# Two additions per unit become one, the context product moves to the start, and loads and products of the first units are reordered

## What is computed

```python
h = gelu(gelu(cond @ W0 + b0) @ W1 + b1)
att = softmax(h @ W2 + b2)                       # (64, 8)
c = einsum('boi,bih->boh', att @ weight, x) + att @ bias_k
q, k, v = c @ Wq, c @ Wk, c @ Wv                 # with their biases; 32 values per row, 32 heads for q only
o = softmax(q * k / sqrt(32)) @ v                # per row; 32 values
x = x + repeat(o, 32 times each)                 # 32 -> 1024 channels
y = conv1d(x, weight, 9 taps, 4 groups) + cond @ c_weight.T + bias
out = x + y @ (scale * (unpack4(packed) - zero)).T + ffn_bias
```

## Time and profile before

| | |
|---|---|
| median of 3 runs | 431.62 us (431.26 to 432.72) |
| the profiled execution | 432.14 us, its span 430.2 us |
| mean granted TensorE clock | 0.992 |
| PE busy | 412.6 us (96%) |
| DVE busy | 363.5 us (85%) |
| POOL busy | 340.9 us (79%) |
| ACT busy | 226.8 us (53%) |
| DMA | 79.05 MB, mean 184 GB/s |

### The profile page before, as it was taken

One profiled execution on the slowest core, in us unless ns is written; L12 is line 12 of the kernel. 1 busy time (PEld: TensorE's weight loads), 2 busy tenths in 40 slices (PEclk: granted clock), 3 DMA queues, 4 the chain that ended last, 5 costly groups with the idle time before them and its releaser, 6 DMA issues.

```text
span 430.2 us, 6661 instructions
## 1 busy us (share of the span) xinstructions
PE 412.6 (96%) x2195; PEld 348.8 (81%) x2195; DVE 363.5 (85%) x603; ACT 226.8 (53%) x465; POOL 340.9 (79%) x316
## 2 busy tenths in 40 slices
PE   3969899899999999999999999999999999999997
PEld 2969799778888888888888888888888888888885
DVE  2896999998989899899989799998989799983421
ACT  3854655556455274657446365647264465562700
POOL 4033948769686999999999979899979979999920
PEclk9988999999999999999999999999999999999999
DMA  8989246470637565664736290928174371816112
GB/s 312 385 330 379 102 149 225 146 270 5 182 106 265 192 220 202 181 240 143 281 100 223 62 350 20 329 88 259 63 237 185 69 254 38 287 41 234 48 52 98
DMA packets 21752, 79.05 MB, mean 184 GB/s; under 512 B 5704, under 2 KB 5832, under 8 KB 17352
## 3 DMA queue, kind: packets, MB, share of 16 engines
q1 hardware_dynamic: 21416, 77.21, 51.2%
q10 hardware_dynamic: 288, 1.18, 0.9%
HBM read 61.11 MB, written 17.27 MB: 182 GB/s over the span
## 4 chain that ended last, share of the span: by engine, by line
PE 79%; DVE 6%; DMA 2%; issue 1%; POOL 1%; ACT 0%; DVEq 0%; POOLq 0%
PE p_f L1159 51%; PE p_conv L1153 19%; PE p_sm L1129 7%; PE p_sm L1138 1%; DMA o_c<-o_dram 1%; DMA o_dram<-o_sb 1%; DVE den L837 1%; DVE c_lo L882 1%; DVE xc L876 1%; DVE prob L828 1%; DVE prob L833 1%; DVE p_sm L845 1%; POOL xc L440 0%; DVE p_ut L893 0%; DVE prob L841 0%
## 5 line engine op out<-in xcount | busy, mean ns | idle before, releaser
L1159 PE MATMUL p_f<-w_ffn,u_hi 128*128 128x512 f32 x512 | 195.8, 392 | 0.0
L1159 PE MATMUL p_f<-w_ffn,u_lo 128*128 128x512 f32 x512 | 194.9, 390 | 0.0
L610 ACT ACTIVATE u_sb<-p_conv,u_bias,cols_sb 128x128 f32<-128x128 f32 x256 | 95.0, 460 | 42.2 <-PE p_conv L1153 40.2
L1159 PEld LDWEIGHTS p_f<-w_ffn,u_lo 128*128 128x128 f32 x512 | 96.2, 188 | 20.5
L1159 PEld LDWEIGHTS p_f<-w_ffn,u_hi 128*128 128x128 f32 x512 | 96.1, 188 | 20.5
L453 POOL TENSOR_TENSOR c_lo<-xc,c_hi 128x516 fp32r<-128x516 f32 (+1 forms) x66 | 82.7, 1263 | 11.6 <-ACT c_hi L600 6.8
L464 POOL TENSOR_TENSOR xn<-xn,bias_n 128x1024 f32<-128x1024 f32 x32 | 76.3, 2403 | 4.7 <-DMA xn<-xn_in_in 4.6
L600 ACT ACTIVATE c_hi<-xc 128x516 fp32r<-128x516 f32 (+1 forms) x68 | 41.0, 608 | 65.0 <-POOL xc L445 59.8
L440 POOL TENSOR_TENSOR xc<-xc,o_c 128x384 f32<-128x384 f32 x60 | 54.3, 905 | 24.5 <-DMA o_c<-o_dram 23.3
L906 DVE TENSOR_TENSOR xn<-p_f,xn 128x512 f32<-128x512 f32 x64 | 43.4, 678 | 23.8 <-PE p_f L1159 23.4
L893 DVE STREAM_TRANSPOSE p_ut<-u_sb 128x512 f32<-128x512 f32 (+1 forms) x68 | 45.8, 680 | 16.4 <-ACT u_sb L610 16.3
(11 more groups left out here) (113 smaller groups left out, 458.6 us busy)
## 6 DMA issues: line engine op xcount, KB each, us to landing
xc<-xc_in_in SPq DMA_DIRECT2D x16, 1032.0 KB, 8.8
xn<-xn_in_in SPq DMA_DIRECT2D x16, 1024.0 KB, 7.1
out<-xn SPq DMA_DIRECT2D x31, 512.0 KB, 7.0
xt<-xt_in_in SPq DMA_DIRECT2D x15, 1024.0 KB, 5.6
o_c<-o_dram SPq DMA_DIRECT2D x15, 256.0 KB
xn<-wq_in SPq DMA_DIRECT2D x4, 512.0 KB, 12.4
xt<-wq_in SPq DMA_DIRECT2D x1, 1024.0 KB, 6.8
xn<-wq_in SPq DMA_DIRECT2D x1, 1024.0 KB, 8.8
```

Source lines behind the costliest of these rows:

```text
L610: ins = eng.activation(u_sb[:, g % 2, i * P:(i + 1) * P], p_conv[g % 2][:, i * P:(i + 1) * P], ACT.Identity, bias=u_bias[:, g, bat:bat + 1 ...
L1159: return mm(p_f[half][:, :], u[:, (k // TU) % 2, r, t * P:(t + 1) * P], w_ffn[:, r, 512 * half:512 * half + 512], **flags)
```

## The change

1. **Context early.** The weights of the context product come with the small inputs (`ctxw`, 64 more columns in `cols`), POOL repeats them eight times into `ctx_sb` right after its fills, and PE computes the product between the third small product and the transpose, into `p_conv[1]`. ACT makes `u_bias` from it right after the small exponential. The load of `ctx_w` is gone. `cbs`, which ACT needs for it, is DVE's first instruction.
2. **Order on PE.** project(1) is in one piece. mix(1) stands behind three quarters of project(2), copy_o(0,0) to (0,2) behind the first quarter of project(3), and the five `keep_busy` are split into two and three. ACT has z_copy(2) ahead of two conversions of weights and the first c_high.
3. **Order of loads.** The conv weights come before x of unit 2, x(2) before xc(0), x(3) before xn(0) and xc(1). x(6) is issued by SP behind spread_o(1).
4. **Edges.** `o_sb` gets a column of zeros on each side of the 32 values. `save_o` writes it a second time, with the zeros (`o_pad`), and `spread_o` reads that back twice, for the lower 64 partitions from element 0 and for the upper ones from element 1, into `cw_o`, which shares its memory with the conv weights. So one addition of 33 values per group and batch (every fourth block from block 0 to 128) does in all partitions what the two additions of 64 partitions did: `add_edges`, once per unit, on DVE for unit 1 and on POOL ahead of add_o from unit 2 on. Per unit on POOL, 8 additions go and 1 comes. `c_low` and `x_bias` lose waits which they don't need any more, `spread_o` gets one for the edges of the unit that used the buffer.
5. The scratch space for DMAs that GpSimd would issue is halved, for the memory.

The diff, cut to its core:

```diff
-            return o_sb[:, (k // TU) % 2, k % TU, :]
+            return o_sb[:, (k // TU) % 2, k % TU, 1:DH + 1]
...
+        def edges(a):
+
+            c = xc[:, a % 2, :, :, :].rearrange("p n g m -> p (n g) m")[:, :, 0:MW:4]
+            return c.rearrange("p (n g) d -> p n g d", g=G), cw_o[:, a % 2, :, 0:DH + 1].rearrange("p (n g) d -> p n g d", g=G)
...
             def spread_o(a):
                 eng.wait_ge(s_ow, 32 * a)
                 eng.wait_ge(s_add, added(max(a - 1, 1), G - 1))
+                if a == 3:
+                    eng.wait_ge(s_edge1, 1)
+                if a > 3:
+                    eng.wait_ge(s_edge, a - 3)
...
+                eng.wait_ge(s_pw, 32 * a)
+                if a == 1:
+                    eng.wait_ge(s_cwl, 1)
+                for h in range(2):
+                    eng.dma_start(cw_o[64 * h:64 * h + 64, a % 2, :, :].rearrange("p k d -> p (k d)")[:, 0:RUN],
+                                  o_pad[a].rearrange("(c e) -> c e", c=CG)[:, h:h + RUN].unsqueeze(0).broadcast_to([R // 2, CG, RUN])).then_inc(s_oe[a % 2], 16)
...
             load_x(1)
+            load_conv_weights()
             load_x(2)
-            load_conv_weights()
-            load_context()
             load_c(0)
-            load_c(1)
+            load_x(3)
             eng.wait_ge(s_w3, 4)
             load_n(0)
-            load_x(3)
+            load_c(1)
...
             def add_o(p, g):
...
-                eng.tensor_tensor(x4[0:64, :, :, 3], x4[0:64, :, :, 3], o[0:64], ALU.add).then_inc(s_add, 1)
-                eng.wait_ge(s_add, added(p, g) - 2)
-                eng.tensor_tensor(x0[64:P, :, :, 0], x0[64:P, :, :, 0], o[64:P], ALU.add).then_inc(s_add, 1)
...
+            def add_edges(p):
+                b = unit_of(p)
+                eng.wait_ge(s_xc[b % 2], 16 * (b // 2 + 1))
+                eng.wait_ge(s_oe[b % 2], 32 * ((b + 1) // 2))
+                c, o = edges(b)
+                eng.tensor_tensor(c, c, o, ALU.add).then_inc(s_edge, 1)
...
             mm(p_sm[0][0:B, 128:128 + KE], h_sb[:, 1, :], w2_sb, start=True, stop=True).then_inc(s_pe0, 1)
+            context()
```

More of the change, by code:

```diff
@@ L36, with block_program @@
 NP = NU + 1
+RUN = UB * G * (DH + 2) - 1
 AT = {}
 NCOLS = 0
-for _name, _n in (("cond", B), ("w0", P), ("w1", P), ("w2", KE), ("b0", 1), ("b1", 1), ("cbias", G), ("scale", 1), ("zero", 1), ("own", 4), ("b2", KE), ("mixb", P), ("brow", W3)):
+for _name, _n in (("cond", B), ("w0", P), ("w1", P), ("w2", KE), ("b0", 1), ("b1", 1), ("cbias", G), ("scale", 1), ("zero", 1), ("own", 4), ("b2", KE), ("mixb", P), ("brow", W3), ("ctxw", G * CG)):
     AT[_name] = slice(NCOLS, NCOLS + _n)
     NCOLS += _n
-def block_program(nc, xt_in, xc_in, cols, mix_w, wq, wvk, conv_w, ctx_w, packed_t, xn_in, bias_in, out):
+def block_program(nc, xt_in, xc_in, cols, mix_w, wq, wvk, conv_w, packed_t, xn_in, bias_in, out):
     ctx = ExitStack()
@@ L88, in block_program @@
         w_ffn = sb("w_ffn", [P, R, D], F32R)
-        cw = sb("cw", [P, 2, G, P])
+        cw_o = sb("cw_o", [P, 2, UB * G, DH + 2])
+        cw = cw_o[:, :, :, :].rearrange("p s k d -> p (s k d)")[:, 0:2 * G * P].rearrange("p (k g o) -> p k g o", k=2, g=G)
         cw_hi = sb("cw_hi", [P, 2, G, P], F32R)
@@ L173, in block_program @@
         o_dram = nc.dram_tensor("o_dram", [NU, CG, UB * G, DH], F32).ap()
+        o_pad = nc.dram_tensor("o_pad", [NU, CG * UB * G * (DH + 2)], F32).ap()
         s_small = sem("s_small")
@@ L192, in block_program @@
         s_oz = sem("s_oz")
+        s_pw = sem("s_pw")
+        s_oe = [sem(f"s_oe{i}") for i in range(2)]
         s_sel = sem("s_sel")
@@ L365, in _ @@
             spread_o(1)
+            load_x(6)
             eng.wait_ge(s_w3, 6)
@@ L509, in _ @@
             c_low(2, 3)
+            add_edges(3)
             add_o(3, 0)
@@ L521, in _ @@
             x_o(5)
+            add_edges(4)
             add_o(4, 0)
@@ L535, in _ @@
             for p in range(5, NP):
+                add_edges(p)
                 add_o(p, 0)
@@ L556, in _, with bias_of_u @@
             eng.activation(att[:, 1, :], att[:, 0, :], ACT.Exp, scale=-1.0, bias=att_s[:, 0:1], accum_out=att_s[:, 1:2]).then_inc(s_act0, 1)
+            def bias_of_u():
+                eng.wait_ge(s_cb, 1)
+                eng.wait_ge(s_cbs, 1)
+                for g in range(G):
+                    eng.activation(u_bias[:, g, :], p_conv[1][:, B * g:B * g + B], ACT.Identity, bias=cbs[:, g:g + 1], scale=sc).then_inc(s_ub, 1)
+            bias_of_u()
             eng.wait_ge(s_wvk, 16)
@@ L596, in c_high @@
                 if p == TU and g == 0:
-                    eng.wait_ge(s_edge, 2)
+                    eng.wait_ge(s_edge1, 1)
+                if p > TU and g == 0:
+                    eng.wait_ge(s_edge, p - TU)
                 if p >= TU:
@@ L661, in _ @@
             u_copy(1, 0)
-            load_x6()
             u_high(0, 3)
@@ L744, in _ @@
             eng.wait_ge(s_small, 16)
+            eng.tensor_scalar(cbs[:, :], cbias_sb, sc, None, ALU.mult).then_inc(s_cbs, 1)
             eng.wait_ge(s_pe0, 3)
@@ L771, in _ @@
             eng.tensor_scalar(zp[:, 1:2], zero, ZLIM, -ZLIM, ALU.min, ALU.max).then_inc(s_zp, 1)
-            eng.tensor_scalar(cbs[:, :], cbias_sb, sc, None, ALU.mult).then_inc(s_cbs, 1)
             eng.wait_ge(s_zp, 1)
@@ L872, in add_edges @@
                 eng.wait_ge(s_xc[1], 16)
-                eng.wait_ge(s_oc[1], 16)
-                for rows, at in ((slice(0, 64), 1), (slice(64, P), 0)):
-                    x = xc[rows, 1, :, :, at:at + P].rearrange("p n g (d j) -> p n g d j", j=4)[:, :, :, :, 3 * at]
-                    eng.tensor_tensor(x, x, o_c[rows, 1, :, :, :], ALU.add).then_inc(s_edge, 1)
+                eng.wait_ge(s_oe[1], 32)
+                c, o = edges(1)
+                eng.tensor_tensor(c, c, o, ALU.add).then_inc(s_edge1, 1)
             def c_low(p, g):
@@ L1199, in context @@
             def context():
-                eng.wait_ge(s_ctx, 16)
+                eng.wait_ge(s_ctx, 1)
                 for g in range(G):
-                    last = mm(p_ut[0][:, B * g:B * g + B], ctx_sb[:, g, :], cond_sb, start=True, stop=True)
+                    last = mm(p_conv[1][:, B * g:B * g + B], ctx_sb[:, g, :], cond_sb, start=True, stop=True)
                 last.then_inc(s_cb, 1)
@@ L1265, in _ @@
             project(1, 1, 0)
-            context()
             project(1, 1, 1)
@@ L1269, in _ @@
             project(2, 0, 1)
+            project(2, 1, 0)
             mix(1)
-            project(2, 1, 0)
             project(2, 1, 1)
+            keep_busy(p_conv[0], 2)
+            project(3, 0, 0)
             copy_o(0, 0)
@@ L1275, in _ @@
             copy_o(0, 2)
-            keep_busy(p_conv[0], 5)
-            project(3, 0, 0)
+            project(3, 0, 1)
+            project(3, 1, 0)
             copy_o(0, 3)
-            project(3, 0, 1)
+            project(3, 1, 1)
             conv(0, 0)
-            project(3, 1, 0)
-            project(3, 1, 1)
+            keep_busy(p_conv[1], 3)
             copy_o(1, 0)
```

53 lines of the change are left out of this document (19 added, 34 removed).

## The result

| | before | changed |
|---|---|---|
| median, us | 432.17 (4 runs) | 442.88 (4 runs, 441.54 to 445.26) |
| ratio, 95% interval | | 1.0255 (1.023 to 1.0281) |
| profiled execution, us | 432.14 | 445.26 |
| its span, us | 430.2 | 443.5 |
| its mean granted clock | 0.992 | 0.984 |

The forecast was 427.1 us and a range up to 430.2. The change is 10.7 us slower in the medians, 13.3 in the two spans. POOL did lose its 38 us of work, and it bought nothing.

A forecast was written before the change was run, and what follows sets the result against it. PE bounds the kernel from 97 to 345 us, so only the start and two short waits can be won. +0.1 - 4.0 + 1.0 - 1.2 - 0.4 = -4.5 us; forecast 427.1 us as a median, range 425.5 to 428.6.

The forecast's parts named there:

- the price of the padded copies: Two more copies behind o_c from unit 2 on: 0.28 MB, 0.7 us at 432 GB/s, with both issues 1.5 us.
- the sum for p=3: Chain from o to the first c_lo at p=3: 13.7 instead of 13.3 us; PE's 0.4 us wait still goes.
- rival 4: Padded copies land late, add_edges first on POOL delays c_lo, PE waits: slower, 434 us for 9 us late; chance 0.05.
- The price is paid once, at the worst unit: Late copies cost PE time at one unit only, since DVE and PE then shift together; passes the gain at 6.5 us.
- x(6) only as a gain for o_c: x(6) no longer travels ahead of o_c, for which POOL waited 7.0 us, so POOL's adds come earlier.
- The stages: From 97 to 345 us PE is busy 248.00 of 248.00 us, so relieving only POOL, DVE or ACT gains nothing.
- both waits for c_lo behind 60 us: PE's waits after 60 us, 1.2 us for DVE's low conv input and 0.4 us for POOL's, both go.
- the whole sum of -4.5: Whole kernel: context +0.1, start order -4.0, blocked subtraction +1.0, PE's two later waits -1.2 and -0.4 us.
- POOL's two splits: Splits of the conv weights, 1.04 and 2.37 us, run from 24.1 to 27.6 us instead of from 28.41.
- rival 2: Clock falls again when PE stands 2.5 us before the second o, by 40.3 us: about 428.6 us; chance 0.17.
- Rival 1: Early conv weights make POOL's split block DVE's second nibble operation; softmax_top(0) about 3.2 us late: 429.3 us; chance 0.13.
- The block of the subtraction by POOL's split: DVE's subtract(0,0), at 26.61 us, waits until 27.6 beside POOL's conv-weight split: +1.0 us, bounds 0 to +3.4.

The follow-up runs named there:

- the start's kernel: Kernel before with only context early, the new orders of PE, ACT and loads, and x(6) on SP; edges as before: 428.82 us, ratio 0.9944.
- the one with both cures: Changed kernel with eight DMAs of 16 partitions per padded copy pair and the edge addition behind the first two middle additions: 431.5 us, ratio 0.9987.

## Why the prediction was wrong

**The step that failed is the price of the padded copies in the sum for p=3, and with it the weight of rival 4.** It took the two padded copies at 1.5 us behind o_c (bytes at 432 GB/s plus their issue), and forecast 13.7 us from o to the end of the first c_lo. Measured: 81.68 to 97.69, 16.0 us. The edge addition began 11.5 us behind o, not 9.4, and took 1.59, not 1.2 us. Bytes over the full rate was the wrong price: these copies ran on 4 of 16 DMA engines, behind o_c, and spread over 16 they made the kernel 10.9 us faster. The prediction also let o(2) come 3.9 to 5.4 us earlier than 81.13 us; in the start's kernel it does (76.61), in the change it came at 81.68, so the sum began late as well. The rival named the right instruction and the right wait, with a chance of 0.05; its threshold, about 2 us behind o_c, fits the medians of 3.9 us in the change and 2.1 with 16 engines. Its evidence against, "the new copies differ from it by 0.28 MB", rested on the same price.

**"The price is paid once, at the worst unit" also failed.** At p=3, the unit that the sum looked at, PE waited only 0.57 us. Behind 60 us it waited for POOL's c_lo eight times, 7.4 us in all, longest 2.6 (at 201.65), and the stretch of 96 to 345 us lost 5.8 us of PE. The rival's 434 us for copies 9 us late was too low; with copies that landed 2.8 to 4.6 us behind o_c the kernel took 442.9.

**Missed: who else stands behind the copies.** DVE's edge addition of unit 1 waited 1.97 us for them; x(6), moved behind them, made PE stand 3.83 us, and behind that the clock was down. The prediction counted x(6) only as a gain for o_c. Undoing x(6) alone gained nothing, since DVE's wait takes its place. In the profiled executions of the change and of the start alone, 18.2 us apart in their spans, 2.4 us are there when the first linear begins (61.54 and 59.16, the half clock of the start); behind it PE's waits are 3.8 us for x(6), 7.4 for c_lo and 1.0 for u_lo, against none.

**What held.** The stages: no gain from POOL's relief. The start, when alone: both waits for c_lo behind 60 us went with it, so the whole sum of -4.5 applies to it. The profiled execution, one of the faster group, was 4.9 us shorter in its span than before's; the median gained 2.6. POOL's two splits ran from 24.17 to 27.68 in the changed kernel (forecast 24.1 to 27.6). The difference between -4.5 and -2.6 is most likely a fall of the clock as in **rival 2**, in about half of the runs. Its chance of 0.17 was too low, its price (1.5 us over the forecast) of the right size, its place only partly right: the rival put it behind a stand at about 40 us; in the changed kernel the clock fell at 23 us already, behind the 1.2 us stand before mix(0), and again at 47, behind stands of 0.96 and 1.56 us. **Rival 1** did not come: the conv weights landed no earlier than forecast, the splits began behind both nibble operations, and these kept their 0.68 us; so its rule was not put to the test. The block of the subtraction by POOL's split was 0.76 us where 1.0 was forecast. The Trainium skill ("SBUF — State Buffer", Who interferes with whom) has a VectorE instruction with two SBUF inputs contend with a GpSimd instruction that reads SBUF, and this trace agrees.

**Open.** Why PE's waits for c_lo differ so much from unit to unit: POOL's 14 waits for the copies vary from 2.2 to 8.9 us, and the size of POOL's wait does not tell PE's (5.9 us ahead of PE's longest, 2.61; 6.9 and 6.1 us in two units in which PE did not wait); no run varied one of the other transfers. Which part of the eight pieces' gain is the number of engines: they are also eight issues in place of two, and no run changed the one without the other. And why the kernel with x(6) ahead of the copies was not faster than the one without.

## What to carry to other kernels

A DMA's price is not its bytes over the full rate: before moving work from an engine onto a second copy, look at how many engines the copy runs on (4 of 16 here, with the repeat of 4 outermost) and at what is queued with it. Ask first whether anybody waits for it: copies just as slow cost nothing unread, and 14 to 15 us with POOL's and DVE's edge additions waiting for them. And when an instruction must wait for a late transfer, let those that need only the early one go first; moving one line behind two was worth 6.8 us here.

## What the runs showed of the hardware

- The 128 packets of 2172 bytes of a unit took 3.2 to 5.3 us as two DMAs of 64 partitions from 4 repeats (4 engines), and 2.9 to 4.8 us as eight DMAs of 16 partitions (16 engines), each beside other transfers. What changed is that the latter overlap o_c.
- An edge addition on POOL, every fourth element, took 1.59 us for 128 partitions x 528 elements and 1.56 us for 64 x 512: half of the partitions saved nothing.
- PE stood 1.2 us ahead of mix(0) in the kernel before, the changed one, the start's, the one with edges from o_c and the one with both cures. In the profiled executions of the second and the last the granted clock was at half behind it (0.50 at 24 to 27 us), in those of the other three it stayed at 1.00.
